# Entry to the second layer and query stage: bias add and norm on GpSimd, scaling on ScalarE, a hand-written VectorE order, queries written in two parts from PSUM

## The chip, the cores and the metric

The kernel runs on one core of a Trainium2 chip. The metric is device time in microseconds (us) of one execution, from the inputs in HBM to the output in HBM. A core has five engines that run side by side and wait for one another through semaphores: TensorE (PE, matmuls and transposes into PSUM), VectorE (DVE), ScalarE (ACT), GpSimd (POOL, which reads and writes SBUF alone) and SyncE (SP, which here issues most DMAs; ScalarE issues the others).

## The reference

Two layers of cross-attention on x (8 batches of 112 tokens, 512 wide) and a context of 375 rows per batch:

```
layer 0: q, k, v = x Wq + bq, ctx Wk + bk, ctx Wv + bv      (32 heads of 16, 8 kv heads)
         x = x + softmax(q k' * 0.25 + mask) v Wo + bo
         x = (x - mean) / sqrt(var + 1e-6) * gamma + beta
layer 1: for i in 1, 2:                                      (16 heads of 128)
         h = layernorm_i(x) * scale_i + offset_i
         q, k, v = h Wq_i + bq_i, ctx Wk_i + bk_i, ctx Wv_i + bv_i; one learned row joins k and v
         x = x + softmax(q k' / sqrt(128)) v Wo_i + bo_i
         x = x + gelu(layernorm(x) W1 + b1) W2 + b2
```

All in float32.

## The kernel before

The eight batches are done in two halves of four (HB = 4, T = 4 x 112 = 448 tokens). For TensorE each float32 operand is split into a high and a low part of the type fp32r; a product is three matmuls, hi hi, hi lo and lo hi (`three`, L650 to L654). One `keys1` unit is 4 x 3 matmuls of 376 columns, a query unit 4 x 3 of 448. Splitting a product means: ScalarE writes the high part from PSUM (`move`, L1008), VectorE writes source minus high part (`lo_of`, L1315; with a bias it is a scalar_tensor_tensor, L1320, else a tensor_tensor, L1318).

A half goes through: keys, queries and values of layer 0; its softmax loop of 128 steps; the output projection with Wo of layer 0 (four units `out_part`, one per batch); two attentions of layer 1 with four groups of four heads each (`attend(a, g)`, so eight groups a half); and the MLP. Each engine has one instruction stream written out by hand in the order in which the other engines need it; PSUM banks `pj` (three) are used round robin by unit number, and a unit waits until `pj_free` counts the unit three before it as freed. So the places of the units in `first_units` (L96) and the order in each engine's block must fit one another.

The stretch that the change is mostly about is the entry from layer 0 into the second layer. After the loop ScalarE issues DMAs of the row bo (into tmp[0]), of four batches of x (into xa) and of gamma and beta (into tmp[1], tmp[2]), L1160 to L1165; the three tmp buffers lie in the tile `probs`. VectorE then does for each batch in turn (L1533 to L1557): x + bo, the projection's result from PSUM added (this frees the bank), bn_stats and aggregate, then (x - mean) * gamma, the reciprocal of the std that ScalarE takes, times that plus beta, and statistics again for the first layer norm. TensorE's first key unit of group 0 waits for the fourth batch's bank. Then VectorE normalizes a batch into tmp[0] (`normed`, L1335), TensorE transposes it, VectorE scales and shifts it from PSUM into tmp[1] with four tensor_scalars (`scaled`, L1344), ScalarE copies tmp[1] to h_hi (`h_parts`, L1027), VectorE subtracts for h_lo (`h_rest`, L1354) and adds the row bo1 to xa (`row_bias`, L1361). Units go k0, k1, k2, x0, k3, x1, x2, x3, and the queries (q0 to q3) follow when all of h is there.

In every attention group and in the MLP the queries go: ScalarE writes bias + scale * PSUM into tmp (L1236), VectorE casts it to qo_hi and subtracts it for qo_lo (`q_stage`, L1376, frees the bank), in the order q0, q1, q2, maximum of head 0, q3, maximum of head 1, normalization of head 0. Then per head: scores on TensorE, maximum on VectorE (L1590), exponential on ScalarE (L1195), reciprocal and multiplication on VectorE (`norm1`, L1598), three transposes on TensorE (`transpose1`, L886).

Weights come chunk by chunk (four of 128x512 per matrix) through the two slots of `raw`: SyncE waits for the slot to be free and issues the load, GpSimd waits for it and for the weight buffer, writes the high part (L576) and the low part (L578), and frees the slot. Wq and Wv share the buffer "b". ScalarE's increment after the last query copy (L1238) lets GpSimd start Wv, the one after the last value copy (L1221) lets it start the next group's Wq. GpSimd's order in a group: Wo, Wv, next Wk, next Wq.

Of the kernel before, what the change touches and what calls it, by code (L numbers as in the profile page):

```python
# [20 lines left out]
HB = B // HALVES  # L21
# [74 lines left out]
def first_units(a, g):  # L96
    left = normed_first(a, g)
    keys = [("k", 0, h) for h in range(HPG)]
    x = [("x", b) for b in left]
    if len(x) == 2:  # L100
        return keys[0:1] + x[0:1] + keys[1:3] + x[1:2] + keys[3:]
    return keys[0:3] + x[0:1] + keys[3:] + x[1:]
# [98 lines left out]
CHAIN_H, STD_H = 2 * HB, HB * (ATT + 2)  # L201
ST_H = (2 + NG) * HB
NL = ATT + 1

# [13 lines left out]
def xattn_program(nc, x, x_t, ctx_t, mask, wq0, wk0, wv0, wo0, wq, wk, wv, wo, w1, w2,  # L218
# [12 lines left out]
    with ExitStack() as ctx:  # L231
# [85 lines left out]
        raw_free = [sem("raw_free0"), sem("raw_free1")]  # L317
        split_hi, raw_scaled = sem("split_hi"), sem("raw_scaled")
# [18 lines left out]
        post_ln, bias_added, stats_ready = sem("post_ln"), sem("bias_added"), sem("stats_ready")  # L337
        mask_in, bo_in, rows_ready, out_done = sem("mask_in"), sem("bo_in"), sem("rows_ready"), sem("out_done")
# [218 lines left out]
        def _(pool):  # L557
# [11 lines left out]
            def split_free(n, shape, hi, lo, signal, k, done):  # L569
# [5 lines left out]
                pool.sem_inc(pool_passed, 1)  # L575
                nc.gpsimd.tensor_scalar(hi, src, 1.0, 0.0, ALU.mult, ALU.add).then_inc(split_hi, 1)  # L576
# [3 lines left out]
                pool.sem_inc(raw_free[slot], 1)  # L580

            def weights(n, name, free, use):
                pool.wait_ge(w_free[name], free + 1)
                for c in range(DC):
                    split_free(n + c, (1, GW), w_hi[name][:, c, :], w_lo[name][:, c, :], w_ready[name], 1,
                               use * DC + c + 1)
# [21 lines left out]
            for hf in range(HALVES):  # L608
# [18 lines left out]
                def queries1(ag):  # L627
                    weights(base + RAW_A + ag * RAW_GU + DC, "b", use_b + B_G + 2 * ag, use_b + B_G + 2 * ag)
# [5 lines left out]
                queries1(0)  # L634
# [372 lines left out]
        def _(act):  # L1007
# [9 lines left out]
            def ln_std(chain, batches, which):  # L1017
                act.wait_ge(ln_chain, chain)
                nc.scalar.activation(std[0:L, batches], mean_var[0:L, batches, 1], ACT.Sqrt,
                                     bias=eps[0:L, which:which + 1]).then_inc(std_ready, 1)  # L1020
# [6 lines left out]
            def h_parts(nl, b, unit):  # L1027

                for k in range(2):
                    if k == 0:  # L1030
                        act.wait_ge(ln_t, nl * HB + b + 1)
# [32 lines left out]
            for hf in range(HALVES):  # L1064
# [65 lines left out]
                for n in range(NT):  # L1130
# [31 lines left out]
                for b in range(HB):  # L1162
                    act.dma_start(xa[0:L, b, :], x[(hf * HB + b) * L:(hf * HB + b + 1) * L, :]).then_inc(x_in[b], 16)
                act.dma_start(probs_flat[0:L, D:3 * D],
                              rows_in[0:1, D:3 * D].partition_broadcast(L)).then_inc(rows_ready, 16)  # L1165
                for b in range(HB):
# [629 lines left out]
```

## Time and profile before

| | |
|---|---|
| median of three runs | 2555.87 us (2555.66 to 2564.72) |
| profiled execution: its own time | 2556.51 us |
| its span, first to last instruction | 2554.7 us |
| TensorE busy | 2329.4 us (91%) |
| VectorE busy | 1506.3 us (59%) |
| ScalarE busy | 998.7 us (39%) |
| GpSimd busy | 698.1 us (27%) |
| mean granted TensorE clock | 0.969 |

Busy times are sums over instructions; an engine that is not busy may still be held, since waits and DMA issues are not counted. A clock of 1.00 is 2.4 GHz throughout, 0.50 would be 1.2 GHz throughout. In a view, `pj<-ctx_hi,wk_hi` reads: written tile, then read tiles.

### The profile page before, as it was taken

Reading aid. Unit: us, or ns where it says so; the run is one execution under the profiler, and the core shown is the slowest. Engines: PE = TensorE matmul, PEld = TensorE weight load, DVE = VectorE, ACT = ScalarE, POOL = GpSimd, SP = SyncE. Lnnn points to the kernel's source line nnn. Section 1 sums busy time; section 2 is a strip of 40 time slices with the busy share of each in tenths; the row PEclk is TensorE's granted clock in tenths of the full one; section 3 lists DMA queues with packets and bytes.
Section 4 is the critical chain, followed back from the end, with each engine's and each line's share of the span. In section 5 each row is a group of like instructions: output and inputs, shape, how many; then the busy total and the mean of one; then the engine's idle time right before and its main releaser. Section 6 shows DMA issues by size and latency. Waiting matters only on the chain. (4 is left out here: it accounts for less than half of the span.)

```text
span 2554.7 us, 36666 instructions
## 1 busy us (share of the span) xinstructions
PE 2329.4 (91%) x13176; PEld 2077.3 (81%) x13176; DVE 1506.3 (59%) x3426; ACT 998.7 (39%) x2271; POOL 698.1 (27%) x734
## 2 busy tenths in 40 slices
PE   4798799999999999998969978999999999999988
PEld 4565698999989898997756657999889898998976
DVE  4697655455575555456538976455555655455564
ACT  2686333332434333243118843342424333242420
POOL 4021213224141313313541211214141313314045
PEclk8899899999999999999989988999999999999999
DMA  5632222232333323223453412232323223223222
GB/s 184 203 113 61 66 87 92 88 103 84 104 99 92 100 75 104 88 91 127 149 160 103 111 49 68 90 95 88 102 94 102 92 79 103 86 91 116 77 69 81
DMA packets 118889, 253.25 MB, mean 99 GB/s; under 512 B 13648, under 2 KB 37232, under 8 KB 117664
## 3 DMA queue, kind: packets, MB, share of 16 engines
q1 hardware_dynamic: 76504, 140.73, 17.9%
q10 hardware_dynamic: 42208, 110.18, 14.0%
q8 instruction: 109, 1.79, 0.3%
q14 instruction: 68, 0.56, 0.1%
HBM read 222.40 MB, written 31.22 MB: 99 GB/s over the span
## 5 line engine op out<-in xcount | busy, mean ns | idle before, releaser
L652 PE MATMUL pj<-ctx_hi,wk_hi 128*128 128x376 f32 x1088 | 380.3, 350 | 36.5 <-DVE xacc L1369 21.6
L653 PE MATMUL pj<-ctx_lo,wk_hi 128*128 128x376 f32 x1088 | 372.7, 343 | 0.0
L654 PE MATMUL pj<-ctx_hi,wk_lo 128*128 128x376 f32 x1088 | 371.5, 341 | 0.0
L1318 DVE TENSOR_TENSOR rr<-pj,rr 128x448 fp32r<-128x448 f32 (+1 forms) x280 | 174.4, 628 | 249.5 <-ACT rr L1011 249.5
L576 POOL TENSOR_SCALAR wk_hi<-raw 128x512 fp32r<-128x512 f32 (+1 forms) x84 | 52.5, 625 | 977.6 <-DMA raw<-in_wk 817.8
L1320 DVE SCALAR_TENSOR_TENSOR k_lo<-pj,cur,k_hi 128x375 fp32r<-128x375 f32 x256 | 155.1, 607 | 247.2 <-ACT k_hi L1013 245.9
L657 PEld LDWEIGHTS tp<-ident,probs 112*125 112x125 f32 (+1 forms) x1536 | 197.9, 165 | 120.4 <-DVE probs L1598 41.9
L652 PE MATMUL pj<-pt_hi,nat 125*128 125x448 f32 x768 | 287.0, 374 | 7.0 <-issue 5.9
L657 PE MATMUL tp<-ident,probs 112*125 112x112 f32 (+1 forms) x1536 | 231.6, 270 | 60.2 <-DVE probs L1598 36.0
L1195 ACT ACTIVATE probs<-scores,prm 112x376 f32<-112x376 f32 x256 | 147.4, 576 | 353.2 <-DVE prm L1590 353.1
L1013 ACT ACTIVATE k_hi<-pj,cur 128x375 fp32r<-128x375 f32 x256 | 146.8, 573 | 353.1 <-PE pj L654 343.3
L654 PE MATMUL pj<-pt_hi,nat 125*128 125x448 f32 x768 | 282.5, 368 | 0.0
L653 PE MATMUL pj<-pt_lo,nat 125*128 125x448 f32 x768 | 282.2, 367 | 0.0
L652 PEld LDWEIGHTS pj<-ctx_hi,wk_hi 128*128 128x128 f32 x1088 | 211.4, 194 | 41.0 <-DVE xacc L1369 23.4
L576 POOL TENSOR_SCALAR wb_hi<-raw 128x512 fp32r<-128x512 f32 x152 | 98.1, 645 | 474.9 <-ACTq L1221 185.3
L1011 ACT ACTIVATE rr<-pj 128x448 fp32r<-128x448 f32 (+1 forms) x280 | 152.3, 547 | 162.0 <-PE pj L654 152.2
L653 PEld LDWEIGHTS pj<-ctx_lo,wk_hi 128*128 128x128 f32 x1088 | 211.3, 194 | 1.2
L654 PEld LDWEIGHTS pj<-ctx_hi,wk_lo 128*128 128x128 f32 x1088 | 210.8, 194 | 0.0
L578 POOL TENSOR_TENSOR wb_lo<-raw,wb_hi 128x512 fp32r<-128x512 f32 x152 | 200.6, 1320 | 12.7
L1318 DVE TENSOR_TENSOR pt_lo<-tp,pt_hi 126x336 fp32r<-126x336 f32 (+1 forms) x384 | 181.3, 500 | 10.0 <-ACT pt_hi L1011 10.0
L1011 ACT ACTIVATE pt_hi<-tp 126x336 fp32r<-126x336 f32 (+1 forms) x384 | 157.8, 448 | 46.6 <-PE tp L657 45.7
L652 PEld LDWEIGHTS pj<-pt_hi,nat 125*128 125x128 f32 x768 | 144.2, 188 | 27.5 <-issue 16.4
(168 smaller groups left out, 5326.9 us busy)
## 6 DMA issues: line engine op xcount, KB each, us to landing
nat<-nat_scratch ACTq DMA_DIRECT2D x256, 384.0 KB, 3.7
raw<-in_wk SPq DMA_DIRECT2D x72, 256.0 KB, 3.8
raw<-in_wq SPq DMA_DIRECT2D x72, 256.0 KB, 3.3
raw<-in_wo SPq DMA_DIRECT2D x72, 256.0 KB, 2.6
raw<-in_wv SPq DMA_DIRECT2D x64, 256.0 KB, 3.3
raw<-in_w SPq DMA_DIRECT2D x64, 256.0 KB, 2.9
nat_scratch<-rr SPq DMA_DIRECT2D x8, 1536.0 KB, 7.0
queries_scratch<-rr SPq DMA_DIRECT2D x32, 224.0 KB
```

The source lines that it names most:

```text
L576: nc.gpsimd.tensor_scalar(hi, src, 1.0, 0.0, ALU.mult, ALU.add).then_inc(split_hi, 1)
L578: nc.gpsimd.tensor_tensor(lo, src, hi.bitcast(F32), ALU.subtract).then_inc(signal, k)
L652: nc.tensor.matmul(dst, l_hi, r_hi, start=first, stop=False)
L653: nc.tensor.matmul(dst, l_hi, r_lo, start=False, stop=False)
L654: return nc.tensor.matmul(dst, l_lo, r_hi, start=False, stop=last)
L657: return nc.tensor.transpose(dst, src, ident[0:parts, 0:parts])
L1011: i = nc.scalar.activation(dst, src, ACT.Copy)
L1013: i = nc.scalar.activation(dst, src, ACT.Identity, bias=bias)
L1195: nc.scalar.activation(probs[0:L, h, 0:SK], scores[n % SCR][0:L, 0:SK], ACT.Exp, bias=neg_max[0:L, h:h + 1], accum_out=row_sum[0:L, h:h + ...
L1318: i = nc.vector.tensor_tensor(dst, src, hi.bitcast(F32), ALU.subtract)
L1320: i = nc.vector.scalar_tensor_tensor(dst, src, bias, hi.bitcast(F32), ALU.add, ALU.subtract)
```

## The change

- Layer 0 to layer 1, bias row: `x + bo` for all four batches is done by GpSimd; VectorE waits for it ahead of each bank add.
- The rows gamma and beta go into the two slots of `raw` (their DMA is issued by ScalarE at step 112 of layer 0's loop, once Wq of group 0 is split; GpSimd does not free the slots until the last of the affine passes is done; the loads of group 0's Wo come after that).
- The norm of the first layer norm (into tmp[0]) is done by GpSimd. The scaling is done by ScalarE, straight from PSUM, twice per 112 columns: once into h_hi, once into tmp[1]; VectorE subtracts from it as before.
- Units of group 0: x0, k0, k1, x1, k2, k3, x2, x3. VectorE's order is a written list (`l0_norms`), in which the bank adds come earlier; the four row-bias adds come last.
- Queries of all sixteen attention groups (not the MLP's): ScalarE writes bias + PSUM to qo_hi, VectorE subtracts from PSUM for qo_lo; tmp isn't used. The factor 1/sqrt(128) is multiplied into each Wq chunk by GpSimd ahead of its split. (The query bias already carried the factor.)
- The first layer norm's sqrt and reciprocal steps have semaphore counts of their own; what is counted is the same.

The core of the diff (left out: semaphore declarations, count changes, code whose only change is its place; in the last list several calls stand on a line):

```diff
+    if len(x) == HB:
+        return x[0:1] + keys[0:2] + x[1:2] + keys[2:4] + x[2:4]
...
# GpSimd
+                if scaled is not None:
+                    nc.gpsimd.tensor_scalar(src, src, SCALE1, 0.0, ALU.mult, ALU.add).then_inc(q_scaled, 1)
+                    pool.wait_ge(q_scaled, scaled)
                 nc.gpsimd.tensor_scalar(hi, src, 1.0, 0.0, ALU.mult, ALU.add).then_inc(split_hi, 1)
...
-                queries1(0)
+                queries1(0, keep=2)
+                pool.wait_ge(bo_in, hf * 16 + 16)
+                for b in range(HB):
+                    pool.wait_ge(x_in[b], hf * 16 + 16)
+                    nc.gpsimd.tensor_tensor(xa[0:L, b, :], xa[0:L, b, :], tmp[0][0:L, :], ALU.add).then_inc(bias_added, 1)
+                pool.wait_ge(bias_added, hf * 16 + HB)
+                nl = hf * NL
+                for b in range(HB):
+                    pool.wait_ge(ln_inv, nl * HB + b + 1)
+                    if b > 0:
+                        pool.wait_ge(pj_ready, PJ_AT[hf]["g", 0, 0] + GU[0][0]["x", b - 1] + 1)
+                    nc.gpsimd.tensor_scalar(tmp[0][0:L, :], xa[0:L, b, :], mean_var[0:L, b, 0:1],
+                                            rstd[0:L, b:b + 1], ALU.subtract, ALU.mult).then_inc(xn_ready, 1)
+                pool.wait_ge(post_ln, (hf + 1) * 2 * HB)
+                for s in raw_free:
+                    pool.sem_inc(s, 1)
...
# ScalarE
+            def x_parts(nl, b, unit):
+                act.wait_ge(pj_ready, unit + 1)
+                act.wait_ge(ln_par, nl + 1)
+                act.wait_ge(ln_lo, (nl * HB + b) * 2)
+                for k in range(2):
+                    for c in (2 * k, 2 * k + 1):
+                        nc.scalar.activation(h_hi[:, c, b * L:(b + 1) * L], pj[unit % PJ][:, c * L:(c + 1) * L],
+                                             ACT.Identity, bias=ln_cur[:, 4 + c:5 + c], scale=ln_cur[:, c:c + 1])
+                    for c in (2 * k, 2 * k + 1):
+                        i = nc.scalar.activation(tmp[1][:, c * L:(c + 1) * L], pj[unit % PJ][:, c * L:(c + 1) * L],
+                                                 ACT.Identity, bias=ln_cur[:, 4 + c:5 + c], scale=ln_cur[:, c:c + 1])
+                    i.then_inc(ln_hi, 1)
...
+                    if n == NT - 16:
+                        act.wait_ge(w_ready["b"], (hf * WB_H + B_G + 1) * DC)
+                        act.dma_start(raw[0:L, :, :], rows_in[0:1, D:3 * D].partition_broadcast(L).rearrange(
+                            "p o (r n) -> p (o r) n", r=2)).then_inc(rows_ready, 16)
...
+                        post_std(hf, 0)
+                        post_std(hf, 1)
+                        ln_stds(nl, 0)
+                        ln_stds(nl, 1)
+                        post_std(hf, 2)
+                        x_in_place(0)
+                        keys1(0, 0)
+                        ln_stds(nl, 2)
+                        post_std(hf, 3)
+                        keys1(0, 1)
+                        x_in_place(1)
+                        ln_stds(nl, 3)
+                        keys1(0, 2)
+                        keys1(0, 3)
+                        x_in_place(2)
+                        x_in_place(3)
...
                     for h in range(HPG):
-                        if h == 1:
-                            act.wait_ge(bias_added, hf * 16 + a * HB + 2 * HB)
-                        if h == 3:
-                            act.wait_ge(pj_free, q_at + 1 + PJ)
-                        act.wait_ge(pj_ready, q_at + h + 1)
-                        nc.scalar.activation(tmp[(h + 1) % 3][:, 0:T], pj[(q_at + h) % PJ][:, 0:T], ACT.Identity,
-                                             bias=cur[:, h:h + 1], scale=SCALE1).then_inc(pj_mid, 1)
+                        move(qo_hi[:, h, :], pj[(q_at + h) % PJ][:, 0:T], pj_ready, q_at + h + 1,
+                             bias=cur[:, h:h + 1], mid=pj_mid)
...
# VectorE
+                    def queries1(h):
+                        name = ("q", h)
+                        lo_of(qo_lo[:, h, :], pj[gu[name] % PJ][:, 0:T], qo_hi[:, h, :], pj_mid,
+                              gmid + gm[name] + 1, pj_free, bias=cur[:, h:h + 1])
...
+                    ln_begin(nl, 0)
+                    added(0); moments_of(0, 0); post_normed(0); added(1); moments_of(1, 0); added(2)
+                    moments_of(0, 1); inverse(0); post_normed(1); added(3); moments_of(1, 1); moments_of(2, 0)
+                    inverse(1); rest(0); post_normed(2); keys1(0); moments_of(2, 1); moments_of(3, 0)
+                    keys1(1); inverse(2); post_normed(3); rest(1); moments_of(3, 1); keys1(2)
+                    inverse(3); keys1(3); rest(2); rest(3)
+                    for b in range(HB):
+                        dve.wait_ge(xn_ready, nl * HB + b + 1)
+                        row_bias(b, hf * 64 + 32)
```

In that list `added` is the bank add, `moments_of(b, 0)` and `(b, 1)` the statistics before and after the affine pair `post_normed`, `inverse` the reciprocal, `rest` the bank's release and `h_rest`, `keys1` the low part of a key.

## Rows read from the trace of the kernel before

**Rows 1.** Windows, entry of half 0: length, busy us and count per engine, clock, DMA.

```profile
238.00:252.00 14.00, 13.44 (x48) 9.75 (x48) 7.67 (x15) 2.17 (x4) 0.00 (x0) 0.82 0.41 115
252.00:261.00 9.00, 0.01 (x1) 0.01 (x1) 7.74 (x16) 0.89 (x3) 0.62 (x1) 0.76 0.00 0
261.00:273.00 12.00, 11.58 (x52) 11.23 (x52) 9.22 (x22) 3.10 (x8) 7.42 (x7) 0.75 0.34 104
273.00:283.40 10.40, 2.40 (x12) 1.50 (x12) 10.17 (x30) 2.80 (x7) 0.00 (x0) 0.70 0.01 4
283.40:295.00 11.60, 11.56 (x48) 10.61 (x49) 3.40 (x7) 1.91 (x3) 0.00 (x0) 0.83 0.00 0
```

**Rows 2.** Timeline, VectorE, half 0: start, us, line, operation, tiles, shape; in brackets idle before.

```profile
242.61 0.69 DVE L1536 TENSOR_TENSOR xacc<-xacc,probs 112x512 f32<-112x512 f32 x1 [4.37 <-DMA xacc<-in_x]
...
244.42 0.69 DVE L1324 BATCH_NORM_STATS2 prm<-xacc 112x6 f32<-112x512 f32 x1
...
246.15 0.75 DVE L1546 SCALAR_TENSOR_TENSOR xacc<-xacc,prm,probs 112x512 f32<-112x512 f32 x1 [0.71 <-DMA probs<-in_rows]
...
247.01 0.75 DVE L1552 SCALAR_TENSOR_TENSOR xacc<-xacc,prm,probs 112x512 f32<-112x512 f32 x1
...
260.24 0.69 DVE L1369 TENSOR_TENSOR xacc<-pj,xacc 112x512 f32<-112x512 f32 x1 [0.18 <-DVE xacc L1536]
...
271.29 1.29 DVE L1348 TENSOR_SCALAR probs<-pj,prm 128x112 f32<-128x112 f32 x4
...
273.14 0.69 DVE L1318 TENSOR_TENSOR h_lo<-probs,h_hi 128x224 fp32r<-128x224 f32 x2
```

**Rows 3.** Timeline, TensorE, half 0: first matmul of the queries.

```profile
283.44 0.71 PE L652 MATMUL pj<-h_hi,wb_hi 128*128 128x448 f32 x1 [2.50 <-DVE h_lo L1318]
```

**Rows 4.** Groups by form, ScalarE: count, busy us, mean ns, idle before and its releaser.

```profile
L1011 ACT ACTIVATE rr<-pj 128x448 fp32r<-128x448 f32 x256 | 138.7, 542 | 152.3 <-PE pj L654 152.2
...
L1236 ACT ACTIVATE probs<-pj,cur 128x448 f32<-128x448 f32 x64 | 40.7, 636 | 130.4 <-PE pj L654 130.4
...
L1013 ACT ACTIVATE rr<-pj,prm 128x112 fp32r<-128x112 f32 x32 | 11.0, 343 | 4.4 <-PE pj L657 4.4
```

**Rows 5.** Timeline, ScalarE, layer-0 steps: two activations one behind the other.

```profile
187.72 0.34 ACT L1013 ACTIVATE rr<-pj,prm 128x112 fp32r<-128x112 f32 x1
187.96 0.44 ACT L1011 ACTIVATE pt_hi<-tp 125x336 fp32r<-125x336 f32 x1
```

**Rows 6.** Timeline, GpSimd: Wq of group 3, first chunk's first pass, last chunk's last.

```profile
612.00 0.63 POOL L576 TENSOR_SCALAR wb_hi<-raw 128x512 fp32r<-128x512 f32 x1 [13.75 <-ACTq L1221]
...
620.51 1.29 POOL L578 TENSOR_TENSOR wb_lo<-raw,wb_hi 128x512 fp32r<-128x512 f32 x1
```

**Rows 7.** Timeline, TensorE, group 3: first matmul of the queries.

```profile
625.33 0.36 PE L652 MATMUL pj<-h_hi,wb_hi 128*128 128x448 f32 x1
```

**Rows 8.** Waits of TensorE: us in all, times, longest.

```profile
PE tp L657 <- DVE probs L1598: 36.0, 28, 2.6
```

**Rows 9.** Timeline, VectorE, group 1, round the end of the queries.

```profile
411.07 0.38 DVE L1379 CAST qo<-probs 128x448 fp32r<-128x448 f32 x1
411.49 1.59 DVE L1318 TENSOR_TENSOR qo<-probs,qo 128x448 fp32r<-128x448 f32 x1
413.00 0.54 DVE L1590 TENSOR_REDUCE prm<-scores 112x1 f32<-112x376 f32 x1
...
417.62 1.23 DVE L1598 TENSOR_SCALAR probs<-probs,prm 112x376 f32<-112x376 f32 x1
```

**Rows 10.** Timeline, ScalarE, group 1: the key copy behind four DMA issues.

```profile
415.85 0.57 ACT L1013 ACTIVATE k_hi<-pj,cur 128x375 fp32r<-128x375 f32 x1 [1.60 <-PE pj L654]
```

**Rows 11.** Timeline, GpSimd, group 1: the first Wv chunk's second part.

```profile
411.11 1.48 POOL L578 TENSOR_TENSOR wb_lo<-raw,wb_hi 128x512 fp32r<-128x512 f32 x1
```

**Rows 12.** Timeline, TensorE, groups 1 and 2: transposes of the second head's probabilities.

```profile
418.91 0.51 PE L657 MATMUL tp<-ident,probs 112*126 112x112 f32 x3 [2.37 <-DVE probs L1598]
...
530.96 0.51 PE L657 MATMUL tp<-ident,probs 112*126 112x112 f32 x3 [1.11 <-DVE probs L1598]
```

More of the change, by code:

```diff
@@ L579, in split_free, with weights @@
                 pool.wait_ge(signal, done)
-                pool.sem_inc(raw_free[slot], 1)
-            def weights(n, name, free, use):
+                if not keep:
+                    pool.sem_inc(raw_free[slot], 1)
+            def weights(n, name, free, use, keep=0, scaled=None):
                 pool.wait_ge(w_free[name], free + 1)
@@ L1015, in move, with post_std @@
                     i.then_inc(mid, 1)
[L1017 to L1020, printed above, removed]
+            def post_std(half, b):
+                act.wait_ge(ln_chain, half * HB + b + 1)
+                nc.scalar.activation(std[0:L, b:b + 1], mean_var[0:L, b:b + 1, 1], ACT.Sqrt,
+                                     bias=eps[0:L, 0:1]).then_inc(std_ready, 1)
+            def x_parts(nl, b, unit):
[10 more added lines that the diff above has]
+                    i.then_inc(ln_hi, 1)
             def ln_stds(nl, b):
@@ L1223, in attend, with x_in_place @@
                     act.wait_ge(cur_ready, hf * CUR_H + a * G1 + g + 1)
-                    for name in first_units(a, g):
+                    if a == 0 and g == 0:
+                        def x_in_place(b):
+                            x_parts(nl, b, gpj + gu["x", b])
+                        post_std(hf, 0)
[14 more added lines that the diff above has]
+                        x_in_place(3)
+                    for name in first_units(a, g) if a + g > 0 else []:
                         if name[0] == "k":
@@ L1374, in out_part, with q_stage @@
                     ln_stat(b)
-            def q_stage(mid0, done0, heads=range(HPG)):
-                for h in heads:
+            def q_stage(mid0, done0):
+                for h in range(HPG):
                     dve.wait_ge(pj_mid, mid0 + h + 1)
@@ L1622, in out1 @@
                             moments(nl + 1, b, st + b + 1)
-                    q_mid, q_done = gmid + gm["q", 0], (hf * (NG + MLPG) + a * G1 + g) * HPG
-                    left = normed_first(a, g)
-                    if len(left) == HB:
-                        ln_begin(nl, a)
-                        normed(nl, 0)
-                    for name in first_units(a, g):
+                    for name in first_units(a, g) if a + g > 0 else []:
                         if name[0] == "k":
@@ L1638, in attend @@
                             row_bias(b, rows)
-                    q_stage(q_mid, q_done, range(3))
+                    for h in range(3):
+                        queries1(h)
                     max1(0, 0)
-                    q_stage(q_mid, q_done, range(3, 4))
+                    queries1(3)
                     max1(0, 1)
@@ L1707, in _ @@
                 group_operands(0)
+                l0_norms()
                 for a in range(ATT):
```

122 lines of the change are left out of this document (82 added, 40 removed).

## The prediction

> **What bounds the kernel now.** The page's first part comes first: TensorE is busy 2329.4 of 2554.7 us, VectorE 59%, ScalarE 39%, GpSimd 27%. So nearly all of the span is matmul time that this change leaves alone, and it can win only where TensorE stands. Two views tell where: the windows of the stretch that the new VectorE order covers, and the waits of TensorE.
>
> The windows show the way from layer 0 into the second layer [rows 1]. The output projection ends at 252 and TensorE then does nothing for nine us (0.01 busy); VectorE is busy for 7.74 of them. Four key units follow, then 10.4 us in which TensorE works 2.40 and VectorE 10.17. The queries start at 283.44 [rows 3]. So VectorE's list of work is the bound from 242.61, when the tokens have landed [rows 2], to 283.44: 40.8 us, twice in the program (once per half; the second half runs the same list).
>
> The waits show the other place: TensorE stands 36.0 us in 28 pieces for a probability tile that VectorE normalizes [rows 8]. These lie in the sixteen attention groups. In each, the first is at the transposes of the second head, 2.37 us in group 1 and 1.11 in group 2, the shortest [rows 12]; none is over 2.6 [rows 8]. The timelines of the other engines show why. GpSimd starts to split Wv as soon as the queries have left PSUM, and its subtraction runs 411.11 to 412.59 [rows 11]; VectorE's subtraction for the fourth query, issued at 411.49, takes 1.59 us and ends only after that, and the maximum of head 1 waits behind it until 413.00 [rows 9]. From there the chain goes through the exponential, four DMA issues on ScalarE that hold the key copy until 415.85 [rows 10], the next maximum and the normalization at 417.62, and so to the wait.
>
> **The change part by part.** *Queries in two parts from PSUM.* Per group, four casts and four subtractions on VectorE become four subtractions that read PSUM; ScalarE does one activation per head as before. A 512-column operation of VectorE with one operand in PSUM took 0.69 at 260.24 [rows 2]; I take that for 448 columns. The fourth query's copy by ScalarE was ready before the first maximum ended, so the maximum of head 1 starts about 413.00 - 1.35 = 411.65: the cast (0.38, its step to the next 0.42 [rows 9]) and the 0.9 by which 1.59 exceeds 0.69 go. All that hangs on it moves 1.35 earlier. What is late next is GpSimd's split of the second and third Wv chunks, which can hold the normalizations (1.23 us at 417.62 [rows 9] is one held so). Bounds of this edit: from 0 (the hold returns in full at the normalization) to 36.0 (all of rows 8). I cap each group's first wait at 1.35: eleven groups have more, five have 1.1 to 1.3, together 11 x 1.35 + 5.8 = 20.7 us. I take 21, since all sixteen fourth subtractions show that same 1.6 us.
>
> The Trainium skill, "SBUF — State Buffer", section "Who interferes with whom", says that GpSimd and VectorE share one pair of ports under an exclusive lock: a VectorE instruction with two SBUF inputs waits for the end of a GpSimd one that reads SBUF, while one with a single SBUF input does not. The 1.59 us agrees; so does the 0.69 at 260.24, beside which GpSimd was working. By that rule the new query subtractions can't be held at all, and the new GpSimd work at the entry will hold VectorE's affine passes; the first is in the 21 above, the second is a rival below.
>
> *Scale inside Wq.* GpSimd multiplies each Wq chunk before it splits it: one more pass of 0.63 and a gap of 0.08, 0.7 us, times four chunks, times sixteen groups = 45 us of GpSimd. It hides behind the two output units and four key units that TensorE runs meanwhile. In group 3, the tightest, the split starts at 612.00 and the last part ends at 621.80 [rows 6]; with 2.8 more it ends at 624.6, and the queries start at 625.33 [rows 7], their last chunk later still. So cover is left: 0.7 us to the start. Cost 0; were the cover gone, each us would count fourteen times. Wo and Wv behind it move up to 2.8 later; Wo is read at the group's end and Wv in its second half, cost 0. ScalarE's new wait for the first Wq stands at its step 112 of layer 0's 128, behind GpSimd's last work for a long time to come: cost 0; were it late, at most the 2.8 of the added passes a half. The rows gamma and beta now land before they are asked for; before, they cost 0.71 [rows 2].
>
> *Entry: VectorE's new order.* Up to the fourth bank add VectorE had everything of three batches in front, and the add came at 260.24, ending 260.93 [rows 2]. Now come in front of it: four bank adds of 0.69 (2.8), three pairs of statistics and aggregate (from 244.42 to 246.15 less the 0.71 wait is 1.0 each: 3.1), two affine pairs (246.15 to 247.76, 1.6 and a gap each: 3.4), and one reciprocal with a hop to ScalarE (0.6). The bias add leaves VectorE, but GpSimd's takes 1.3 (the subtraction of two SBUF operands at 620.51 [rows 6]), so the start is 243.9: 243.9 + 9.9 = 253.8. GpSimd's adds of batches 1 to 3 run till 247.8 and meet the first affine pair; I put 1.4 us for it. The fourth add ends about 255.2, 5.7 earlier.
>
> After it, before: 283.44 - 260.93 = 22.5 us. After: two statistics pairs, 2.1, to 257.3; ScalarE's work on x0; then on VectorE a pair of h_lo (0.69 [rows 2]), affine pair 1.7, key 0.6, two statistics 2.1, wait for the key copy 0.9, key 0.6, affine pair 1.7, h_lo 0.7, statistics 1.0, the std by ScalarE and its key copy 0.9, two keys and a reciprocal 1.3: 12.2 in all. On ScalarE stand x0 in front of it and x2, x3 behind it, and these are the new price: eight activations of 128x112 a batch, with a pointer for bias and one for scale. One with a pointer for bias took 343 ns; a pointer more is 636 - 542 = 94 ns by the two forms of 448 columns; two in a row overlapped by 0.10 (187.72 to 187.96 is 0.24) [rows 4, 5]. So 0.33 each, 2.7 us a batch. x0 adds 3.2 with its hops. At the end x2 runs while VectorE ends its keys and adds 2.1, x3 follows with 2.7 and h_lo 0.7, with hops 3.7. From 257.3: 3.2 + 12.2 + 2.1 + 3.7 = 21.2, so 278.5; contention with GpSimd's norms 0.2: queries at 278.7 instead of 283.44, 4.7 a half, 9.4 together. The scaling that VectorE loses (1.29 [rows 2]) is paid by 2.7 on ScalarE, which is why 40.8 us shrink by so little. The four row-bias adds come behind the queries' start, 2.7 us under the first query unit's 2.9 (48 matmuls in 11.6 [rows 1]) and ScalarE's copy; if that cover went, 1 us. Bounds: each activation at 0.24 (the spacing in rows 5) instead of 0.33 gives 0.7 x 3 = 2.1 more and no contention 1.6 more, so +8.4 a half; each at 0.44 (no overlap) costs 0.9 x 3 = 2.7, and 2 more of contention makes it 0 a half.
>
> *TensorE's clock.* It was 0.75 in the window after the nine idle us and 0.83 in the queries' [rows 1], so it spends part of each at 1.2 GHz. The keys now start after some 4 idle us, and wait for banks anyway; I count nothing.
>
> Sum: the profiled execution took 2556.5 us (span 2554.7 and 1.8 around it), 0.6 over the median of 2555.9. Less 21 and 9.4: 2526.1, and 2525.5 on the median's scale. I say 2526.
>
> **The rivals.** (a) *The normalization stays late.* GpSimd still splits Wv at that point, and the DMA issues on ScalarE stay between; the hold of 1.23 at 417.62 speaks for it, that the whole chain starts 1.35 earlier against. Then only the entry pays: 2556 - 9 = 2547. (b) *The entry gives nothing*: ScalarE's 24 activations at the end of three batches, and GpSimd's adds holding VectorE's passes as the skill's lock says. By the bound above 0 a half: 2556 - 21 = 2535. (c) *Both give all*: 8.4 a half and 30 of the 36.0: 2556 - 47 = 2509. (d) *Slower: Wq comes too late.* Place: the chunk's three passes on GpSimd at each of the fourteen group borders inside a half. Price: if the new pass costs not 0.7 but what GpSimd's two-input pass takes with its gap, 1.29 + 0.3 = 1.6, Wq is ready at 621.8 + 6.4 = 628.2, 2.9 after the queries' start, 1.1 of it hidden before the last chunk is read at about 627.1. It decides from 1.3 us a pass; at 2 us late or more, with the DMAs of chunks 2 and 3 later too, 14 x 4 = 56, less 30: 2582. The similar pass at 612.00 took 0.63, which speaks against. (e) *The change doesn't do what it says*: VectorE's hand order stalls on a ScalarE step standing behind another, 10 us a half; 2556 - 21 + 20 = 2555, no change.
>
> **How the numbers follow.** The forecast 0.46, (a) 0.13, (b) 0.16, (c) 0.12, (d) 0.06, (e) 0.07. Half a per cent is 12.8 us, about what a measurement of this kernel can tell. Faster holds the forecast, (b), (c) and some of (a): 0.78; same is most of (a) and (e): 0.15; slower (d) and a rest of (e): 0.07. Bounds of the sum: 2508 with the upper ends, 2551 where little comes; that leaves out (d), the worst of (e) and the extreme of (c).
>
> **What would show it.** Queries of half 0 start at 278.7 in the timeline (276 to 282); eight activations a batch at 0.33 spacing; the fourth bank add near 255. In each group no VectorE subtraction of a query over 0.75, the maximum of head 1 about 1.3 us nearer to the fourth query's end, and the waits of TensorE for the normalized tile down from 36.0 to about 15. No wait of TensorE for Wq. I am wrong if those 36.0 stay over 28, if the queries start at 283 or later, or if GpSimd's Wq releases TensorE anywhere.

## Result: 1.3% faster, as forecast

The changed kernel takes 2524.46 us (median of four runs, 2519.47 to 2529.01) against 2555.76 for the kernel before (four runs, 2553.51 to 2564.72). The ratio is 0.9871, 95% interval [0.9856, 0.9887]. Forecast: 2526.0. The profiled execution took 2519.47 us, its span is 2517.7, 37.0 less than the 2554.7 of before. It was the fastest of the four, 5 us under their median, so the windows below add up to 5.7 us more than the medians' 31.3. A second profile of the same kernel (`f1_changed_again` below) has a span of 2524.3.

The first part of the page, changed kernel (busy us, share of the span, instructions):

```profile
span 2517.7 us, 36640 instructions
PE 2315.6 (92%) x13176; PEld 2064.2 (82%) x13176; DVE 1429.0 (57%) x3314; ACT 1011.9 (40%) x2319; POOL 761.2 (30%) x814
```

VectorE lost 77 us of work, GpSimd gained 63 with 80 instructions more (64 Wq passes, eight bias adds, eight norms), ScalarE 13.

Where the time went is read best from windows cut at the same events in both kernels: start of the output projection of layer 0, start of the queries of the second layer, and the same in the second half (layer 0 of the second half, between the third row and the fourth, is left out). First the kernel before, then the changed one (length; busy us and count of PE, PEld, DVE, ACT, POOL; clock; DMA share; GB/s):

```profile
0.00:238.30 238.30, 175.75 (x1053) 134.94 (x1053) 170.53 (x530) 153.63 (x338) 51.58 (x70) 0.92 0.47 143
238.30:283.44 45.14, 27.43 (x112) 22.52 (x113) 34.60 (x80) 8.95 (x21) 8.04 (x8) 0.76 0.22 64
283.44:1315.74 1032.30, 975.19 (x5485) 894.24 (x5485) 571.38 (x1135) 349.30 (x794) 310.15 (x322) 0.98 0.32 100
1499.26:1544.12 44.86, 26.05 (x112) 21.35 (x113) 34.52 (x80) 8.95 (x21) 8.04 (x8) 0.77 0.22 65
1544.12:2554.70 1010.58, 963.30 (x5424) 882.80 (x5424) 552.73 (x1112) 336.60 (x777) 292.31 (x296) 0.99 0.29 90
```

```profile
0.00:235.88 235.88, 174.50 (x1052) 134.08 (x1052) 170.01 (x531) 153.34 (x338) 54.06 (x74) 0.91 0.47 145
235.88:276.05 40.17, 25.14 (x113) 20.46 (x113) 23.50 (x53) 16.36 (x45) 18.73 (x13) 0.85 0.19 54
276.05:1296.94 1020.89, 969.84 (x5484) 888.84 (x5485) 543.28 (x1106) 348.73 (x794) 328.12 (x354) 0.99 0.33 102
1479.64:1520.02 40.38, 25.61 (x113) 20.81 (x113) 23.82 (x53) 16.35 (x45) 18.97 (x13) 0.84 0.17 54
1520.02:2517.70 997.68, 959.01 (x5424) 879.40 (x5424) 525.81 (x1083) 336.07 (x777) 310.81 (x328) 0.99 0.31 92
```

The two entries gave 45.14 - 40.17 and 44.86 - 40.38, together 9.5 us. The stretches with the attention groups gave 11.4 and 12.9, together 24.3. Layer 0 holds the other 3.2 (2.4 ahead of the first entry, 0.8 in the second half). That part is no gain: in the profiles of the eleven kernels with the new entry the first projection starts anywhere from 234.9 to 240.0, in the three with the old one at 238.1 to 238.3. The 24.3 has chance in it too: cut the same way, f1 gives 7.6 and 11.2, together 18.8.

One length repeats much better: from the first matmul of the queries in group 0 to that in group 7, both halves together. It is 1595.7 us in the kernel before and 1577.6 in the changed one, and 1577.7 to 1578.5 in four more profiles with the same instructions in the groups (e1, f1, f3, g2). I call it the groups' length below. (e2, with the groups of before, has 1602.0, at a clock of 0.99 as before.)

The waits of TensorE in the changed kernel (us in all, times, longest), beside [rows 8], where the third of these lines stood at 36.0:

```profile
PE pj L685 <- issue: 20.8, 34, 1.2
PE pj L690 <- POOL probs L663: 15.8, 5, 4.1
PE tp L690 <- DVE probs L1637: 5.8, 16, 0.4
PE pj L685 <- DVE xacc L1429: 1.8, 2, 0.9
```

The last line, the wait for a bank add, was in the kernel before

```profile
PE pj L652 <- DVE xacc L1369: 21.6, 4, 10.6
```

The reader should see four things: 30.2 us of waits for the normalized probabilities are gone; a line that names no engine has grown from 8.2 (22 times, at most 0.9) to 20.8; at the two entries the wait of the first key unit for the fourth bank, 19.8 of those 21.6, is gone; and part of that came back there, since TensorE waits 15.8 for GpSimd's norms where it waited 11.7 for VectorE's, and 10.4 for the last h_lo ahead of the queries where it waited 5.0. No line names GpSimd's wb: TensorE is never released by the split of Wq.

Around the end of the queries of group 1, VectorE, as in [rows 9]:

```profile
401.71 0.67 DVE L1381 SCALAR_TENSOR_TENSOR qo<-pj,cur,qo 128x448 fp32r<-128x448 f32 x1
402.31 0.54 DVE L1629 TENSOR_REDUCE prm<-scores 112x1 f32<-112x376 f32 x1
406.49 0.42 DVE L1637 TENSOR_SCALAR probs<-probs,prm 112x376 f32<-112x376 f32 x1
```

The fourth subtraction takes 0.67 where it took 1.59, there is no cast, and the maximum of head 1 follows it directly. The 64 subtractions of the sixteen groups have a mean of 0.68 and a longest of 0.69: none is held, though 37 of them began while GpSimd was at work. (By the Trainium skill, "SBUF — State Buffer", section "Who interferes with whom", a VectorE instruction with at most one SBUF input, outside the performance modes that use both ports, does not contend with GpSimd; the trace agrees.) One SBUF input alone is not enough, and here the prediction's account of that page is too short: the normalization (a tensor_scalar) reads a single tile in SBUF, and the one at 417.62 in [rows 9] was held to 1.23; casts in the kernel before took up to 1.39 beside GpSimd and 0.39 otherwise. Whether these ran in such a mode no row here shows.

### The profile page after: what moved, and what is told of

Read it like the earlier page. It is cut to its first block and busy times, and to the rows that moved or that the text cites. A ratio compares the mean times of both kernels' runs of the same rounds, so it can differ in the third digit from the quotient of the medians.

```text
span 2517.7 us, 36640 instructions
## 1 busy us (share of the span) xinstructions
PE 2315.6 (92%) x13176; PEld 2064.2 (82%) x13176; DVE 1429.0 (57%) x3314; ACT 1011.9 (40%) x2319; POOL 761.2 (30%) x814
## 5 line engine op out<-in xcount | busy, mean ns | idle before, releaser
L690 PE MATMUL tp<-ident,probs 112*125 112x112 f32 (+1 forms) x1536 | 228.2, 269 | 33.1 <-DVE pt_lo L1379 20.1
L1381 DVE SCALAR_TENSOR_TENSOR qo<-pj,cur,qo 128x224 fp32r<-128x224 f32 (+1 forms) x192 | 101.2, 528 | 205.9 <-ACT qo L1046 205.9
L1046 ACT ACTIVATE qo<-pj,cur 128x224 fp32r<-128x224 f32 (+1 forms) x192 | 97.8, 510 | 238.1 <-PE pj L687 130.2
```

Of the source, the lines that this page charges most:

```text
L690: return nc.tensor.transpose(dst, src, ident[0:parts, 0:parts])
L1046: i = nc.scalar.activation(dst, src, ACT.Identity, bias=bias)
L1381: i = nc.vector.scalar_tensor_tensor(dst, src, bias, hi.bitcast(F32), ALU.add, ALU.subtract)
```

## The experiments

The theory after the result: the entry and the queries' part are independent, and the second comes from GpSimd's hold on VectorE (a hold is an instruction that lasts longer because GpSimd is at work beside it), not from the cheaper instructions. What the 12.6 us in the unnamed wait are was open.

### Each part alone

`e1_queries_only` is the kernel before with the queries written from PSUM and the factor in Wq; `e2_entry_only` has the new entry and the old queries:

```diff
 # e1 against the kernel before (ScalarE, then VectorE)
-                        nc.scalar.activation(tmp[(h + 1) % 3][:, 0:T], pj[(q_at + h) % PJ][:, 0:T], ACT.Identity,
-                                             bias=cur[:, h:h + 1], scale=SCALE1).then_inc(pj_mid, 1)
+                        move(qo_hi[:, h, :], pj[(q_at + h) % PJ][:, 0:T], pj_ready, q_at + h + 1,
+                             bias=cur[:, h:h + 1], mid=pj_mid)
...
-                    q_stage(q_mid, q_done, range(3, 4))
+                    queries1(3)
```

e2 is the changed kernel with these lines the other way round and without the pass over Wq.

> The kernel before with only the queries' part of the change: two parts written from PSUM, the factor inside Wq; the entry from layer 0 stays as it was. Theory: the two parts of the change act apart, and this one brings what lies between the entries in the trace of the changed kernel, 24 us: 2556 - 24 = 2532, and both entries stay at 45 us from the projection's first matmul to the queries'. Rival: the groups got shorter because something shifts with the new entry (the Wo and Wv loads start later after it), then this is 2545 or more.

Measured 2535.76 us, ratio 0.9908 [0.9887, 0.993] to the kernel before at 2559.59 (23 runs), so -23.5.

> The changed kernel with the queries made as before (ScalarE to tmp with the scale, cast and subtraction on VectorE, no factor in Wq). Theory: only the two entries are shorter, 5.0 and 4.5 us: 2556 - 9.5 = 2546, and TensorE's waits for the normalized tile are 36 us again. Rival: the entry is worth nothing in time (its gain comes from a clock state of the one profiled run) and this is 2555.

Measured 2550.16, 0.9965 [0.9953, 0.9976], so -9.0; the entries took 39.9 and 41.2 us. Waits of TensorE, e1 and then e2:

```profile
PE pj L657 <- issue: 19.4, 33, 1.2
PE tp L662 <- DVE probs L1603: 5.9, 16, 0.4
```

```profile
PE tp L687 <- DVE probs L1639: 37.3, 24, 2.6
PE pj L682 <- issue: 8.1, 22, 1.0
```

The parts add up: 0.92% and 0.35% are 1.27%, the whole has 1.29%. The fall of the one wait (36.0 to 5.9 in e1, 37.3 in e2) and the growth of the other (19.4 in e1, 8.1 in e2) both belong to the queries' part.

### The Wq pass: what it costs, and how far its cover goes

```diff
 # e3: no pass (the queries lack the factor)
-                    nc.gpsimd.tensor_scalar(src, src, SCALE1, 0.0, ALU.mult, ALU.add).then_inc(q_scaled, 1)
-                    pool.wait_ge(q_scaled, scaled)
 # e4: three passes a chunk
+                    for i, f in enumerate((SCALE1, 1.0, 1.0)):
+                        nc.gpsimd.tensor_scalar(src, src, f, 0.0, ALU.mult, ALU.add).then_inc(q_scaled, 1)
+                        pool.wait_ge(q_scaled, 3 * (scaled - 1) + i + 1)
```

> The changed kernel without GpSimd's pass that multiplies Wq (so the queries lack the factor 1/sqrt(128)). Theory: the pass is hidden behind the key units and costs 0; 2524, within 3 us of the changed kernel. Rival: GpSimd's 64 passes hold VectorE through the shared ports, or make Wo and Wv late, for some 0.6 us a group: 2514.

Measured 2519.73, 0.9847 [0.9826, 0.9869]; the interval overlaps that of the changed kernel, so the medians alone don't decide between 0 and a few us. The two spans don't either: 2517.6 and 2517.7 are equal, but the second is of the changed kernel's fastest run. The groups' length says more: 1573.6 in the one profile without the pass, 1577.6 to 1578.5 in the five with it. So the pass is not free; it costs some 4 to 5 us in all, between the theory's 0 and the rival's 10. TensorE waits for Wq in neither. Most of the difference stands in the unnamed wait, which is 15.8 without the pass and 19.4 to 20.8 with it: nine large waits instead of thirteen or fourteen, of the kind explained below. By which way the pass makes them more frequent was not tried.

> The changed kernel with three passes over each Wq chunk instead of one (by the factor, then twice by 1.0): 1.4 us more per chunk. Theory (the prediction's rival d): Wq is then 5.6 us later than with one pass, at 630.2 in the place of 624.6 for queries that start at 625.3, so TensorE waits for GpSimd at each of the 14 group borders, about 3.5 us, 49 in all: 2573. Rival: the DMA waits between the chunks take up part of the passes and the last chunks are read later, 2 us a border: 2552; if there is more cover than I worked out, 2530.

Measured 2549.92, 0.9971 [0.9957, 0.9985]: near the rival's 2552, not 2573. Its waits:

```profile
PE pj L686 <- POOL wb_lo L593: 23.3, 14, 2.0
PE tp L691 <- DVE probs L1638: 14.4, 24, 1.3
PE pj L686 <- issue: 9.9, 25, 0.8
```

Fourteen waits, one at each group border inside a half, 1.7 each: the place and the count of rival (d) are right, and the price exists once the cover is gone. With one pass of 0.62 us there are none. The other two lines moved as well; that the place of Wv's split sets them is a guess at this point, which the next experiments take up.

### The unnamed wait: the theory of late context rows

In the changed kernel the large ones stand before the first `pj<-pt_hi,nat` of a group. I took them for late context rows (`nat`), which ScalarE loads just before; `f2_nat_early` issues these loads among the queries' copies. Beside it stand the changed kernel again (`f1`), a shorter way for ScalarE at the entry (`f3`: scaling once from PSUM into tmp[1], then h_hi copied from it in two pieces), and both (`f4`).

```diff
 # f2
                         move(qo_hi[:, h, :], pj[(q_at + h) % PJ][:, 0:T], pj_ready, q_at + h + 1,
                              bias=cur[:, h:h + 1], mid=pj_mid)
+                        if h < 2:
+                            load_nat(0, 2 * h)
+                            load_nat(0, 2 * h + 1)
...
-                    for c in range(DC):
-                        load_nat(0, c)
 # f3
+                for k in range(2):
+                    act.wait_ge(x_scaled, (nl // NL * HB + b) * 2 + k + 1)
+                    nc.scalar.activation(h_hi[:, 2 * k:2 * k + 2, b * L:(b + 1) * L],
+                                         tmp[1][:, 2 * k * L:(2 * k + 2) * L].rearrange("p (c l) -> p c l", c=2),
+                                         ACT.Copy).then_inc(ln_hi, 1)
```

> The changed kernel once more, as the yardstick of this chip: 0.987 of the kernel before. All theories expect the same of it.

> The changed kernel with one edit: the four loads of the first batch's context rows (nat) of a group are issued by ScalarE after the first two query copies instead of after the second exponential. Theory: they are what is late next. In the changed kernel TensorE waits 0.7 to 1.2 us for them in twelve of the sixteen groups (its waits without a releaser grew from 8.2 to 20.8 us), and the issues hold ScalarE's key copy for 1.7 us. Then those 20.8 fall to some 9 and the time by 12 us, 0.5%. Rival: the wait is for something else (the last part of pt_lo, blocked by GpSimd's Wv split), and the time stays within 3 us.

> The changed kernel with ScalarE's work on each normalized batch made smaller: four scaling activations into tmp[1] and two plain copies of 224 columns to h_hi, six instructions instead of eight. Theory: ScalarE's work per batch stands in the entry's chain three times a half; 2.65 us become 4 x 0.33 + 2 x 0.3 + a hop of 0.1 = 2.1, so each entry gets 1.5 us shorter, 3 us in all, and the two copies' results come late enough that h_lo can't start sooner. Rival: VectorE's list sets the entry, and the entry's length stays 40.2.

> Both edits together: the sum of the two, 15 us or 0.6% under the changed kernel if both theories hold; 12 us if only the early loads count.

| | us (median) | ratio to before (2559.13) | 95% | entries, us |
|---|---|---|---|---|
| f1_changed_again | 2524.14 | 0.9862 | 0.9841 to 0.9882 | 40.3, 40.3 |
| f2_nat_early | 2516.20 | 0.9823 | 0.9798 to 0.9849 | 40.4, 41.1 |
| f3_copy_x | 2522.29 | 0.9850 | 0.9826 to 0.9874 | 38.7, 38.4 |
| f4_both | 2507.31 | 0.9798 | 0.9774 to 0.9822 | 38.8, 38.6 |

f3's entries are 1.8 us shorter each, near the 1.5 expected; its whole time cannot be told from the changed kernel's. f2 is 7.9 us under f1 where 12 were expected, and the two intervals overlap a little; the groups' length, 1566.0 against 1578.5, shows the gain clearly, and f4's interval lies clear of f1's. The unnamed wait fell back to 7.6. But the reason I had given for it is wrong, and the cause that I had put down as the rival, pt_lo held by the Wv split, is right (its time, no change within 3 us, is not). Group 1 of the changed kernel, all engines, only the rows round the wait:

```profile
412.45 0.62 POOL L590 TENSOR_SCALAR wb_hi<-raw 128x512 fp32r<-128x512 f32 x1 [1.45 <-DMA raw<-in_wv]
413.14 1.52 DVE L1637 TENSOR_SCALAR probs<-probs,prm 112x376 f32<-112x376 f32 x1
413.15 1.29 POOL L592 TENSOR_TENSOR wb_lo<-raw,wb_hi 128x512 fp32r<-128x512 f32 x1
414.58 0.91 DVE L1379 TENSOR_TENSOR pt_lo<-tp,pt_hi 126x336 fp32r<-126x336 f32 x2
415.59 0.45 PE L685 MATMUL pj<-pt_hi,nat 125*128 125x448 f32 x1 [1.19 <-issue]
```

The matmul starts 0.1 after VectorE's `pt_lo`, the low part of the transposed probabilities, ends (415.49). That stood behind a normalization of 1.52 us instead of 0.42, which began within 0.01 of GpSimd's subtraction for the fourth Wv chunk and ended 0.2 after it. So the unnamed wait is the same hold, one batch further on. It is no single case: the changed kernel has fourteen such waits of 0.70 to 1.22 us (13.1 in all), in fourteen of the sixteen groups, and ahead of each one a normalization took 1.03 to 1.55 with that fourth subtraction beside it. In f2, f4, g1 and g3 no wait at this matmul is over 0.4, and in g1 the context rows are not loaded earlier.

What f2 really moved is the Wv chunk. All 64 loads of a Wv chunk in the changed kernel and in f2, with the median us from issue to landing at the end:

```profile
raw<-in_wv SPq DMA_DIRECT2D x64, 256.0 KB, 4.2
```

```profile
raw<-in_wv SPq DMA_DIRECT2D x64, 256.0 KB, 3.1
```

In group 1 of the changed kernel ScalarE issues the context rows' four loads from 402.88 to 404.20, and the third and fourth Wv chunk, issued at 403.04 and 405.33, take 5.6 and 6.9 us to land. In f2 the rows' loads are issued from 394.96 to 397.80, and the same two chunks take 2.9 and 3.1. The fourth is then split 18.0 us after the start of the group's queries instead of 21.8 (from 410.28 instead of 412.45), mostly ahead of that normalization. The first two chunks, now the ones beside the rows, are slower instead: 4.3 and 3.6 on average over the groups, where they had 3.0 each. So a load of a Wv chunk takes longer when the rows' loads were issued beside it; how the two share the DMA engines no run shows. f2 fell short of removing the hold, though: the wait for the normalized tile rose from 5.8 to 11.4.

### The hold itself

If GpSimd's split of Wv is the cause, moving that split alone, in the kernel before, should bring the queries' gain with no VectorE instruction changed. ScalarE gives the buffer "b" free; the experiment puts that one line later:

```diff
 # g1 (the kernel before) and g3 (f4 and this)
                     # after the four queries
-                    act.sem_inc(w_free["b"], 1)
...
                         exps1(b, 1)
+                        if b == 1:
+                            act.sem_inc(w_free["b"], 1)
```

> The kernel before with one edit: ScalarE's release of the weight buffer after the queries comes later, behind the second batch's first exponentials, so GpSimd's Wv split starts some 20 us later and runs beside none of the first head's work. The queries are still cast and subtracted from tmp. Theory (the hold through the port): the fourth subtraction falls from 1.59 to 0.63 and the normalization from 1.2 to 0.42, so of TensorE's 36.0 us of waits for the normalized tile at least 15 go, and the time is 2556 - 15 = 2541. Rival (number of instructions on VectorE): cast and subtraction are still there, nothing but their length in the profile changes, the waits stay over 30 and the time within 5 us.

Measured 2526.76 (2522.91 to 2530.79), 0.9863 [0.9838, 0.9887] to 2560.98: -35, which is as much as the whole change. The groups' length is 1569.7, 8 us under the changed kernel's. Its waits, and group 1 with VectorE and then GpSimd:

```profile
PE pj L652 <- issue: 7.2, 19, 0.8
PE tp L657 <- DVE probs L1599: 6.2, 18, 0.4
```

```profile
407.30 0.38 DVE L1380 CAST qo<-probs 128x448 fp32r<-128x448 f32 x1
407.72 0.62 DVE L1319 TENSOR_TENSOR qo<-probs,qo 128x448 fp32r<-128x448 f32 x1
408.26 0.54 DVE L1591 TENSOR_REDUCE prm<-scores 112x1 f32<-112x376 f32 x1
412.44 0.42 DVE L1599 TENSOR_SCALAR probs<-probs,prm 112x376 f32<-112x376 f32 x1
```

```profile
421.82 0.63 POOL L576 TENSOR_SCALAR wb_hi<-raw 128x512 fp32r<-128x512 f32 x1 [20.74 <-ACTq L1261]
```

Cast and subtraction of two SBUF operands are all there, and the subtraction takes 0.62 where it took 1.59 [rows 9]. The entries are those of before (44.5 and 45.1). The split of Wv now starts 14.1 us after that subtraction. One moved line takes the 36.0 down to 6.2, and the unnamed wait stays low at 7.2. I had expected 15 us or more. The moved line also lets the loads of the third and fourth Wv chunk start later (from 423.90), away from the context rows', so g1 doesn't part the split from its loads; but TensorE's wait names VectorE, and VectorE's instructions are the ones that became short.

> The changed kernel with the four bias adds back on VectorE, all four in front of its list; the norm stays on GpSimd. Theory: moving the adds to GpSimd won little: the adds cost VectorE 2.6 us in a time in which it mostly waits for the tokens, GpSimd's start cost 1.3 and held the first affine pair for 0.9. The entry is then 0 to 1 us longer than 40.2, and the time within 2 us of the changed kernel. Rival: the full 2.6 us of adds appear in each entry: 43 us, 5 us in all.

```diff
 # g2: the changed kernel, bias adds on VectorE again, ahead of its list
-                    nc.gpsimd.tensor_tensor(xa[0:L, b, :], xa[0:L, b, :], tmp[0][0:L, :], ALU.add).then_inc(bias_added, 1)
+            nc.vector.tensor_tensor(xa[0:L, b, :], xa[0:L, b, :], tmp[0][0:L, :], ALU.add).then_inc(bias_added, 1)
```

Measured 2524.87, 0.9862 [0.9837, 0.9887], entries 41.1 and 41.7, some 1 us longer each. VectorE at its entry:

```profile
239.03 2.85 DVE L1793 TENSOR_TENSOR xacc<-xacc,probs 112x512 f32<-112x512 f32 x4 [3.63 <-DMA xacc<-in_x]
243.45 0.75 DVE L1764 SCALAR_TENSOR_TENSOR xacc<-xacc,prm,raw 112x512 f32<-112x512 f32 x1
```

The four adds cost 2.85 us there but the affine pass is not held (0.75 against 1.29 below). On GpSimd they take 5.49 (shown in the next section); moving them is worth about 1 us a half, which the whole time does not show.

> The version with early context loads and six instructions per normalized batch, and the Wv split started later as in the first kernel of this call. Theory: what is left of the waits for the normalized tile (12.0 us) comes from normalizations held by the Wv split, and some 8 of it go: 2500. Rival: the later split holds other VectorE work of the second batch just as long, and the time is that of the version without it, within 3 us.

> The version with early context loads and six instructions per normalized batch once more, beside the one with the late Wv split on one chip: 0.980 of the kernel before, as measured.

g3 took 2501.22 (2496.87 to 2504.09), 0.9761 [0.9737, 0.9786]: the lowest median, 2.4% under the kernel before. g4 took 2506.07, 0.9787 [0.976, 0.9814]; the intervals overlap, and 4.9 us came where 8 were expected. The traces show the late split's gain: the groups' length is 1559.6 in g3, 1565.9 in f4 and 1567.2 in g4, and the wait for the normalized tile 5.8 against 12.0 and 13.2. g3's waits:

```profile
PE pj L690 <- POOL probs L663: 14.5, 6, 3.7
PE pj L685 <- issue: 7.4, 19, 1.0
PE tp L690 <- DVE probs L1641: 5.8, 16, 0.4
```

Both waits of the groups are at their low level at once, which neither f2 nor the changed kernel reached. g3's span (2502.3) is 23.0 under g1's; the entries (77.0 against 89.6) are 12.6 of it. The other 10.4 lies in the groups (1559.6 against 1569.7) and may be the queries' shorter way or the earlier rows; that stays open. One number points to the rows: TensorE's wait for `pt_lo` is 20.2 in g1 and 14.2 in g3, and over all runs it is 19.6 to 20.5 in the seven that have this late row load and no held query subtraction (the changed kernel, e1, e3, f1, f3, g1, g2; e4, with its waits for Wq, has 17.6) and 13.5 to 14.7 in the four with early rows.

## Why the prediction was right

*The queries' part: forecast 21, came 24.3 by the windows and 23.5 by e1.* The mechanism was right, and g1 shows it: GpSimd's Wv split held the fourth subtraction. The first link came as forecast: the maximum of head 1 in group 1 starts 11.7 us after the group's queries, 13.0 before, so 1.33 earlier against my 1.35. The rest of the size was off in two places that nearly cancel, which is luck. I capped each group's first wait at 1.35, for the hold and the cast; in fact the later waits went with it, and the line fell by 30.2 instead of 21. What I had named as late next came too, but at another place than I looked: not the second and third chunk at the normalizations of batch 0, but the fourth at a normalization of batch 1, and 12.6 us came back. That leaves 17.6. TensorE's busy time in the same stretches fell by 9.6 (975.19 to 969.84 and 963.30 to 959.01) for the same matmuls, at a clock of 0.99 where 0.98 stood in the first. The two make 27.2, which is 2.9 more than the 24.3; the wait for `pt_lo`, up from 16.6 to 20.1, takes about that much back. The clock, which I counted at 0, was a small gain in this profile; how much of it belongs to the change is open, since f1, with the same instructions, gained 5.5 less in these stretches.

*Crediting the cast.* 0.4 of my 1.35 was the cast (with the 0.9 that makes 1.32, not 1.35). g1 keeps all casts and has the gain in full, so that share was wrong in its reason: with the hold gone, the cast lies in time that costs nothing.

*The 0.69 at 260.24* is poor evidence that an instruction with one SBUF operand isn't held, since GpSimd's pass began only at 260.38, behind it. The trace of before has better: 62 of the 104 bank adds, which read PSUM and one SBUF tile, began while GpSimd was at work, and none took over 0.70.

*The Wq pass: forecast 0, cost 4 to 5.* GpSimd in group 1 of the changed kernel:

```profile
376.39 0.62 POOL L588 TENSOR_SCALAR raw<-raw 128x512 f32<-128x512 f32 x1 [13.27 <-ACTq L1268]
```

0.62 against the 0.63 I took from [rows 6]; rival (d) needed 1.3. The cover held for Wq itself: no wait names it, and e4 shows the price behind the cover. What I had put at nothing, the effect on what follows, was small but not nothing: e3's groups are 4.0 us shorter.

*The entry: forecast 9.4, came 9.5 (e2: 9.0), by errors that cancel.* From the start of the projection to the queries I had 278.7 - 238.3 = 40.4; measured 40.17 and 40.38. Inside it, these held: ScalarE's activations from PSUM come in pairs at 0.33 (253.83 to 254.49 is 0.66 for two), 2.8 a batch with the last one's end; VectorE's fourth bank add ended 16.1 us after the projection's start, 16.9 forecast; from it to the first h_lo passed 4.8, forecast 5.3; and from there to the fourth key's end (268.31) 11.5, forecast 12.2. What did not hold is the tail, from there to the queries: 7.7, forecast 6.0. VectorE and GpSimd of the changed kernel, first half:

```profile
243.10 1.29 DVE L1767 SCALAR_TENSOR_TENSOR xacc<-xacc,prm,raw 112x512 f32<-112x512 f32 x1
244.96 1.12 DVE L1773 SCALAR_TENSOR_TENSOR xacc<-xacc,prm,raw 112x512 f32<-112x512 f32 x1
251.31 0.68 DVE L1429 TENSOR_TENSOR xacc<-pj,xacc 112x512 f32<-112x512 f32 x1
274.20 1.55 DVE L1379 TENSOR_TENSOR h_lo<-probs,h_hi 128x224 fp32r<-128x224 f32 x2 [3.09 <-DVEq L1784]
275.67 4.40 DVE L1423 TENSOR_TENSOR xacc<-xacc,probs 112x512 f32<-112x512 f32 x4
```

```profile
240.05 5.49 POOL L655 TENSOR_TENSOR xacc<-xacc,probs 112x512 f32<-112x512 f32 x4 [31.39 <-DMA xacc<-in_x]
249.74 2.42 POOL L663 TENSOR_SCALAR probs<-xacc,prm 112x512 f32<-112x512 f32 x1 [4.21 <-DVE prm L1778]
273.94 1.26 POOL L592 TENSOR_TENSOR wo_lo<-raw,wo_hi 128x512 fp32r<-128x512 f32 x1
```

GpSimd's norm takes 2.08 to 2.50 us (eight, mean 2.27) where my sum had only 0.2 for it, as contention; the waits of TensorE for it (15.8) stand in place of 11.7 for VectorE's, and no run shows what it costs on the path. In the first half ScalarE starts the last batch's activations (271.23) not when the norm has ended (269.98) but when the h_lo before it has (271.11). And the hold is at work here too: the first affine passes (1.29 and 1.12 against 0.75; I had 1.4 for all contention, these two cost 0.9), the last h_lo (1.55, two normally take 0.69) and the four row-bias adds (4.40, forecast 2.7, against 2.85 in g2 for the same kind). The last is hidden under the first query unit, as forecast; the h_lo one, 0.9 too long, is on the path and is half of what the tail has too much. TensorE's share of the gain is in the windows too: clock 0.76 to 0.85 and busy time 27.43 to 25.14 for the same matmuls, 2.3 us in the first half and 0.4 in the second (26.05 to 25.61) that I had at nothing.

*The rivals.* (a) and (b) are excluded by the waits and the entries. Half of (c) was nearer than its 0.12 says: it asked for 30 of the 36.0, which came, and was undone by a wait in another place; its 8.4 a half at the entry did not come. (e) did not occur: no VectorE instruction at the entry waits for a ScalarE step of another batch for long. *The total* came within 1.5 us of the forecast (2524.46 against 2526), nearer than its terms deserve: the old waits fell by 9 more than I had, 12.6 came back elsewhere, the Wq pass cost 4 to 5, and the rest is clock and chance of this profile. That nearness is luck; the two mechanisms, and the two gains of some 20 and 9, are not. *The tells:* queries at 276.05 are just inside 276 to 282, but 2.4 of the distance is the earlier start of the projection; the fourth add at 252.0 is early by 3.2, of which the same 2.4. The 36.0 went to 5.8, not to about 15.

## What to carry to other kernels

A VectorE instruction that lasts two or three times its usual time beside GpSimd's is a limit of its own: look at when GpSimd's work is released before shortening VectorE's. Releasing a weight buffer as early as possible can put the split of the next weights on the tightest chain; one moved line, which puts the split 14 us behind the fourth query's subtraction instead of beside it, brought as much as rewriting the entry and the queries. Where a wait names no engine, look at what ended just before it: here it was the removed hold again, one batch on. And where whole times scatter by more than the effect, compare a stretch between two fixed events that repeats: it showed 4 us of the Wq pass that the spans of two profiles hid.

## What the runs showed of the hardware

- GpSimd's pass with two per-partition operands (subtract, multiply) over 112x512 took 2.08 us in the four cases in which no VectorE instruction with two SBUF tiles ran beside it and 2.41 to 2.50 in the four in which some did; with two constants over 128x512 a pass takes 0.62.
- A VectorE instruction held by GpSimd's subtraction of a weight chunk ends a fixed time after it, by its form: the normalization of 376 columns 0.21 us (the 1.52 at 413.14, GpSimd's end at 414.44; 0.28 in a few), a cast of 448 columns 0.25, the subtraction of 448 columns 0.48 (before: 413.08 against 412.59), a pass over 512 columns 0.55. Alone they take 0.42, 0.39, 0.63 and 0.69. So at most 0.2 us of the instruction's own time goes by during the hold.
- Not every hold lasts to the end of GpSimd's instruction: beside the norm of 249.74 to 252.16, VectorE's second affine pass at 250.32 took 1.07 instead of 0.75 and ended at 251.39, 0.77 before the norm. The rule that the prediction cites from the Trainium skill, that such an instruction waits for the end of GpSimd's, does not hold for this one.
- The third and fourth Wv chunk of a group (256 KB) took 5.5 and 6.8 us on average to land beside the 384 KB loads of context rows, and 3.0 and 3.1 with those loads issued 6 to 8 us earlier.
